# A message-passing kernel whose gathers and scatters are regrouped: from one scatter, one gather to eight scatters, eight gathers

## The reference, cut to what matters

```
emb = _radial_embedding(edge_length)
w = (silu(silu(emb @ mlp_w0 + b0) @ mlp_w1 + b1) @ mlp_w2 + b2).reshape(-1, 4, MUL)
ss, vv = xs[senders], xv[senders]                # gather, one row of x an edge
m0, m1, m2, m3 = ...                             # products of w, ss, vv and the direction
msg_s = segment_sum(mid_s, receivers)            # scatter-add
msg_v = segment_sum(mid_v, receivers)
out = concatenate([msg_s @ W_out0, einsum(msg_v, W_out1)])
x = _layernorm(x + out / 16)
```

## Time and profile before

| | |
|---|---|
| median of 3 timed runs | 1309.8 us (1307.04 to 1310.17) |
| the profiled execution, its own time | 1309.32 us |
| its span, first to last instruction | 1307.5 us |
| GpSimd busy | 1009.7 us, 77% |
| TensorE busy | 1002.6 us, 77% |
| VectorE busy | 698.0 us, 53% |
| ScalarE busy | 541.3 us, 41% |

### The profile page before, as it was taken

The page is one execution under the profiler, slowest core; times in us unless marked ns, Lnnn a source line. Parts: engine busy times, 40 slices in busy tenths (PEclk is TensorE's granted clock), DMA queues, the critical chain, the costliest instruction groups (busy, mean ns, idle before and its releaser), DMA issues.

```text
span 1307.5 us, 29142 instructions
## 1 busy us (share of the span) xinstructions
PE 1002.6 (77%) x6210; PEld 931.8 (71%) x6210; DVE 698.0 (53%) x2916; ACT 541.3 (41%) x1416; POOL 1009.7 (77%) x797
## 2 busy tenths in 40 slices
PE   1878788878788787787868878787877878878770
PEld 1768677777677687777767868776877778767670
DVE  6654434365557456546644655646545736646522
ACT  5423233344535434525524534344443544543431
POOL 4248888888888888888888888888888888888885
PEclk9977877787878777878877887778777777777875
DMA  6456663343443453444444344344344354344434
GB/s 192 153 164 161 160 179 64 67 95 61 103 97 68 96 120 69 96 101 89 94 98 94 71 100 116 70 96 106 68 109 100 66 120 96 68 94 122 85 47 87
DMA packets 83833, 132.08 MB, mean 101 GB/s; under 512 B 16743, under 2 KB 68725, under 8 KB 83003
## 3 DMA queue, kind: packets, MB, share of 16 engines
q0 software_dynamic: 68464, 50.58, 27.6%
q1 hardware_dynamic: 14496, 78.09, 16.7%
q10 hardware_dynamic: 683, 1.38, 0.3%
HBM read 78.35 MB, written 77.24 MB: 119 GB/s over the span
## 4 chain that ended last, share of the span: by engine, by line
issue 48%; POOL 31%; DMA 9%; SPq 5%; POOLq 5%; PE 2%; DVE 1%; ACT 0%; ACTq 0%; DVEq 0%
POOL sender L567 20%; POOL acc L597 11%; DMA acc<-msg,index 6%; SPq L374 3%; POOLq L573 2%; DMA sender<-in_x_dram,index 1%; SPq L370 1%; DMA acc<-in_x_dram 1%; SPq L398 1%; POOLq L595 1%; PE ps_msg L737 1%; POOLq L577 0%; POOLq L596 0%; POOLq L578 0%; PE ps_sum L725 0%
## 5 line engine op out<-in xcount | busy, mean ns | idle before, releaser
L597 POOL DMA_INDIRECT acc<-msg,index x391 | 618.9, 1583 | 120.3 <-issue 113.8
L567 POOL DMA_INDIRECT sender<-in_x_dram,index x380 | 387.2, 1019 | 165.8 <-issue 102.4
L725 PEld LDWEIGHTS ps_sum<-same,mid 128*128 128x128 f32 x1568 | 267.9, 250 | 10.0 <-DVE mid L1148 0.8
L725 PE MATMUL ps_sum<-same,mid 128*128 128x128 f32 x1568 | 270.0, 330 | 0.7 <-DVE mid L1148 0.7
L737 PE MATMUL ps_msg<-outw,sumT 128*128 128x64 f32 x1568 | 241.1, 321 | 0.0
L684 PE MATMUL ps_sT<-ident,sender 128*128 128x128 f32 x381 | 87.6, 304 | 196.9 <-DMA sender<-in_x_dram,index 194.6
L737 PEld LDWEIGHTS ps_msg<-outw,sumT 128*128 128x128 f32 x1568 | 237.6, 239 | 0.0
L822 ACT COPY sumT<-ps_sum 128x512 f32<-128x512 f32 x196 | 114.9, 586 | 268.9 <-PE ps_sum L725 188.2
L1126 DVE TENSOR_TENSOR proj<-ps_up,vec_all 128x384 f32<-128x384 f32 x98 | 54.5, 556 | 313.1 <-PE ps_up L705 258.5
L684 PEld LDWEIGHTS ps_sT<-ident,sender 128*128 128x128 f32 x381 | 50.4, 146 | 222.1 <-DMA sender<-in_x_dram,index 219.2
L1133 DVE TENSOR_TENSOR wts<-ps_wts,bias 128x512 f32<-128x512 f32 x98 | 67.7, 691 | 228.4 <-PE ps_wts L712 189.8
(11 more groups left out here) (144 smaller groups left out, 1035.6 us busy)
## 6 DMA issues: line engine op xcount, KB each, us to landing
acc<-in_x_dram SPq DMA_DIRECT2D x40, 625.0 KB
total<-acc SPq DMA_DIRECT2D x30, 832.0 KB
out_dram<-normed SPq DMA_DIRECT2D x29, 832.0 KB
by_row<-in_x_dram SPq DMA_DIRECT2D x1408, 0.5 KB
acc<-msg,index POOLq DMA_INDIRECT x391
sender<-in_x_dram,index POOLq DMA_INDIRECT x380
out_dram<-normed ACTq DMA_DIRECT2D x1, 832.0 KB
total<-in_edge_attr_dram SPq DMA_DIRECT2D x1, 576.0 KB
```

Of the source, the lines that this page charges most:

```text
L567: pool.indirect_dma_start(sender[:, u % SRING, i, :], None, x, bass.IndirectOffsetOnAxis(ap=index[:, u, 0, i:i + 1], axis=0)).then_inc(fet ...
L597: pool.indirect_dma_start(acc, bass.IndirectOffsetOnAxis(ap=index[:, v, 1, i:i + 1], axis=0), msg[:, v % RING, i, :], None, compute_op=ALU.add
L725: mm = pe.matmul(ps_sum[r][:, i, h, :], mid[:, b, 2 * r + i, P * h:P * (h + 1)], same[:, b, 2 * r + i, :], start=True, stop=True)
```

## The change

GpSimd's order alone is changed. AHEAD is 5 instead of 6. Of the first gathers, each from n = 8 on waits for the one two numbers before it (APART = 2) instead of one. After them the units go in rows of ROW = 2: the scatters of unit v and of unit v + 1 (eight), then the gathers of units v + 5 and v + 6 (eight), with the values of the next two units' orders read between the two groups. The other engines' programs are as they were. The number of scatters and of gathers is the same: 20 first gathers instead of 24 (less the skipped one), four more in the loop. In the row v = 92 only unit 97 is left to be gathered, and the last two rows are scatters alone.

```diff
--- before.py
+++ after.py
@@ -38,8 +38,10 @@
 FULL = E // ROWE
 TILES = UNITS * G
 PAIRS = UNITS // 2
-AHEAD = 6
+AHEAD = 5
+ROW = 2
 APACE = 8
+APART = 2
 RING = 8
 SRING = 16
 SKIPPED = G + 1
@@ -601,27 +603,26 @@
             pool.wait_ge(index_first, 1)
             for u in range(AHEAD):
                 for i in range(G):
-                    if G * u + i >= APACE:
-                        before = G * u + i - 1
-                        if before == SKIPPED:
-                            before -= 1
-                        pool.wait_ge(*fetched(before // G, before % G))
+                    n = G * u + i
+                    of = n - APART
+                    if n >= APACE and of != SKIPPED:
+                        pool.wait_ge(*fetched(of // G, of % G))
                     gather(u, i)
             pool.wait_ge(index_in, 1)
             pool.wait_ge(spare_rows, 16)
             pool.wait_ge(scatter_tables, 1)
-            order = order_of(0)
-            for v in range(UNITS):
-                following = order_of(v + 1) if v + 1 < UNITS else None
-                u = v + AHEAD
-                begin_scatters(v, order)
-                if SRING <= u < UNITS:
-                    pool.wait_ge(senderT_ps, u - SRING + 1)
-                for i in range(G):
-                    scatter(v, i, order % 2)
-                    if u < UNITS:
+            orders = [order_of(v) for v in range(ROW)]
+            for v in range(0, UNITS, ROW):
+                for k in range(min(ROW, UNITS - v)):
+                    begin_scatters(v + k, orders[k])
+                    for i in range(G):
+                        scatter(v + k, i, orders[k] % 2)
+                orders = [order_of(w) for w in range(v + ROW, min(v + 2 * ROW, UNITS))]
+                for u in range(v + AHEAD, min(v + AHEAD + ROW, UNITS)):
+                    if u >= SRING:
+                        pool.wait_ge(senderT_ps, u - SRING + 1)
+                    for i in range(G):
                         gather(u, i)
-                order = following
 
 
         @block.tensor
```

## The result

| | before | after |
|---|---|---|
| median | 1309.65 us (1307.04 to 1310.17, 4 runs) | 1270.63 us (1268.24 to 1272.97, 4 runs) |
| profiled execution | 1309.32 us, span 1307.5 | 1268.24 us, span 1266.2 |

The ratio of the times is 0.9706, 95% interval 0.9679 to 0.9733: faster by about 39 us, where some 45 were forecast.

What follows compares the result with a forecast made beforehand. GpSimd's queue of indirect DMAs was taken as the bound: 78.5 us to the second row, 1171 of work, 10.5 of tail and 1.8 outside give 1261.8; 3 for waits make 1265 us. Forecast range 1247 to 1275 (0.58); whole range 1245 to 1291.

Steps and rivals of the forecast that it cites:

- What sets the pace: Whole kernel: GpSimd's queue of indirect DMAs sets the pace from first scatter (86.94 us) to last (1296.98 us).
- The first gathers: Start: with two gathers in flight the 20th starts at 41 to 50 us instead of 69.02.
- Rival 2: Start: pairs in flight bring nothing because bulk copies fill the DMA engines; 1281 us at most, chance 0.10.
- The first row: First seven scatters from 55.4 us, after the first message, then eight gathers; second row starts at 78.5 us.
- The work left: From 78.5 us: 384 scatters at 1.857 us, 353 gathers at 1.256, plus 5.5 and 9, together 1171 us.
- rival 1: Steady rows: runs bring no cheaper DMAs, so 23 us are not saved; 1287 us, chance 0.13.
- The end: After the last gather: 16 scatters, unit 97's messages in time, tail unchanged at 10.5 us; span 1260.0.
- (a): Each row: the odd unit's message is copied at 25.9 us and wanted at 32.4, a cover of 6.5 us.
- (b): TensorE: two units take 20.5 of a row's 25.0 us, leaving 4.5 us of slack a row.
- rival 4: TensorE becomes the bound through long units after gaps; slower, 1311 us or 1357 us, chance 0.07.
- (c): Scatter n waits for n-4, 7.4 us back instead of 12.8; it lands in 3.19 us, beside bulk 5.07.
- Rival 3: Runs wait: scatters beside bulk, or an odd message now and then, cost 25 to 45 us; 1290 to 1305, chance 0.09.

Runs made afterwards that it cites:

- e3: The changed kernel with each first gather waiting for the one before it (APART 1 instead of 2): 1280.74 us, ratio 0.9792 to the kernel before.
- e7: The changed kernel with each scatter waiting for the one three before it to land instead of four: 1291.69 us, ratio 0.9882 to the kernel before.
- e8: The changed kernel with four first gathers in flight instead of two (APART 4): 1267.23 us, ratio 0.9681 to the kernel before.
- e2: The changed kernel's start alone, followed by the old order of one scatter and one gather in turn: 1285.58 us, ratio 0.9834 to the kernel before.
- e1: The changed kernel's rows of two units alone, with the old start (AHEAD 6, APART 1): 1290.24 us, ratio 0.9861 to the kernel before.
- e6: The changed kernel with four units gathered ahead instead of five (AHEAD 4): 1537.31 us, ratio 1.1758 to the kernel before.
- e9: The changed kernel measured once more, word for word: 1268.55 us, ratio 0.9692 to the kernel before.

## Why the prediction was right

**What sets the pace.** Right. GpSimd's queue stands back to back in both kernels, and only what shortened it or started it sooner moved the time.

**The first gathers.** Right: the 20th starts at 44.13 us, forecast 41 to 50. Rival 2, by which the full DMA engines give a second gather nothing, is out: e3 is 10 to 12 us slower with one in flight. The Trainium skill, page "DMA: Bandwidth & Descriptors", section "Issuing engines are not separate DMA queues", states that DMAs of the scalar, sync and gpsimd engines run on the same 16 DMA engines and interleave. The traces agree that they get in each other's way: scatters land late beside copies (the waits of 3.68 and 2.79 us above, e7). That a second gather in flight would then bring nothing was rival 2's inference from it, and that failed: with one, two and four in flight the 20th gather starts at 63.85 (e3), 44.13 and 33.90 us (e8), beside the same copies.

**The first row.** The place was right, the sizes were not. The first message came 4 us sooner (the first scatter at 51.5, not 55.4), which is luck in part: with the same programs on the other engines the first message was there at 53.05 in e8 and at 53.12 in e2, and the 55.1 of before, from which I counted, is the latest of all the traces. On the other side the two landing waits, 6.5 us together, had no term. The two errors work against each other. I had looked at `far` = 4 with 7.4 us of room and passed over that it is 3 in the first two units, the very place where the copies run. The second row starts at 80.80, forecast 78.5.

**The work left.** From 80.80 to the end of the last scatter at 1255.23 are 1174.4 us, forecast 1171 and 3 for waits. The sum is nearer than its parts: the waits behind the first row are 1.1 us, not 3, and the switches cost more than was put down. The split of the saving into 23 and 27 us was 2.5 too high in sum: by the same prices the old order's last scatter would end at 1299.3, and it ended at 1296.98. The forecast doesn't use it. The term that no steady row of before showed, the gather in a run, is 0.95 as taken from the first gathers; rival 1 is out by e1 and by the rows above. The switch between kinds, 0.12 us a row in the sum, is 0.2 by the rows: 1.62, 1.57 and 1.02, 0.98 against 1.55 and 0.95.

**The end.** 1255.23 to 1266.2 is 11.0 us, forecast 10.5; a wait of 1.01 us stands at 1240.6, behind the last gathers. It is for unit 96's message, whose copy ends at 1239.43; I had followed unit 97's alone, and that one came 4.1 us before it was wanted.

**The waits.** (a) right, 6.4 us against 6.5 at the row shown and 6.3 in the median, though 3.8 at its shortest, and e6 shows what lies behind it. (b) right: TensorE waits 209.0 us for gathers, so it is not the bound, and rival 4 did not come. (c) right in the result, wrong in the size. The landing beside a bulk transfer was taken as 5.07 us from one piece of the chain in the earlier trace rows, and that scatter's own semaphore has a count as late as 5.96 us after its start. Longer ones stood in the same trace. By the last count of each scatter's semaphore, from 200 to 1200 us, 11 of 306 scatters of before landed later than 5.07 us after their start, the longest at 6.97; of the changed kernel 23 of 320, the longest at 6.58. The median is 3.20 before and 3.34 after. So the runs made the landings little longer. What they took is the room, 7.4 us instead of 12.8. A wait that holds also adds about 1 us of release. Rival 3, which I gave 0.09, was nearer than that: one step less of `far` costs 21 to 23 us (e7).

**The whole.** 1270.63 against 1265. In the profiled execution's own terms, 1268.24: 2.3 us in the first row, 0.4 in the work, 0.5 in the tail, and the rest, 2.4 us, lies between that execution and the median, which the sum left out (0.5 before; in e9 0.4, with a median of 1268.55).

## What to carry to other kernels

Where one engine issues DMAs back to back, read the price of a DMA behind one of its own kind and behind one of the other kind as two prices; here the first is 5% less for gathers, and it may show only at the ends of the trace. Before you reorder, follow each buffer's chain back to the transfer that releases it and write down the cover in us; 6.4 us were enough here, and one unit less of lead cost 21% (e6 against the changed kernel). A landing time beside bulk traffic spreads, here from 3 to 8 us, so don't take it from one row: look for the longest in the trace, and check every wait on a DMA "n before", its special cases too, against the new spacing.

## What the runs showed of the hardware that was not expected

- GpSimd's DMA instructions get cheaper over three of a kind in a row: gathers 1.02, 0.98, 0.95 us, scatters 1.62, 1.57, 1.55.
- A wait that really holds GpSimd costs about 1 us of release. From the end of ScalarE's copy to the DMA's start it is 0.97 to 1.22 us (50.53 to 51.50 in the changed kernel, 610.94 to 612.10 and 630.79 to 632.01 in e6), from the last count of a landing 0.8 to 1.0 us (67.92 to 68.73 and 61.40 to 62.43 in the changed kernel). A DMA that waits for nothing starts 0.30 us behind the last. So a release that comes only a little late costs more than it is late by.
- The first message, made by the same programs, came at 50.5 us in the changed kernel and at 55.1 before. TensorE's first matmuls were shorter: `ps_wts` 1.16 us for eight in the changed kernel where before they took 2.08 us in the timeline. The granted clock reads 1.00 from 40 to 44 us in both, and from 32 to 36 us it is 1.00 before and 0.50 in the changed kernel, so it doesn't tell. The change alone isn't the cause: e9, the changed kernel again, has 50.7 with a granted clock of 1.00 from 28 to 48 us, e8 53.05 and e1 52.8. What makes the difference stays open.
